# A decoder layer whose five engines get a new order of calls, with scores, norms and one cast written in another form

## The reference

```python
h = layernorm(x)                                   # self-attention: 16 heads of 16, rotary, causal
q, k, v = h @ Wq.T, h @ Wk.T, h @ Wv.T             # 256 x 256 each
x = x + softmax(mask(rope(q) @ rope(k).T / 4)) @ v @ Wo.T
h = layernorm(x)                                   # cross-attention: 16 heads of 64
Q, K, V = h @ W_Q, ctx @ W_K, ctx @ W_V            # 256 -> 1024
s = where(mask, -1e9, Q @ K.T / 8)                 # 256 x 77 for each head
x = x + softmax(s) @ V @ W_O
h = layernorm(x)                                   # FFN, weights rounded to 8 bits by one scale each
h = gelu(h @ q8(W_fc).T + b_fc + 2 * (h @ A_fc.T) @ B_fc.T)          # 256 -> 1024
x = x + h @ q8(W_proj).T + b_proj + 2 * (h @ A_proj.T) @ B_proj.T    # 1024 -> 256
```

## Time and profile before

| what | value |
|---|---|
| three runs | 632.3, 636.84, 644.2 us; median 636.84 |
| profiled execution | 640.39 us, span 638.6 us, mean granted TensorE clock 0.942 |
| TensorE | busy 528.9 us, 83% of the span, 4334 matmuls |
| VectorE, ScalarE, GpSimd | busy 394.3 (62%), 301.3 (47%), 249.0 us (39%) |
| DMA | 62.45 MB; share of 16 engines 34.8% in the SP queue |
| chain that ended last | PE 54%, DVE 23%, ACT 8%, issue 5%, DMA 5%, POOL 3% |

### The profile page before, as it was taken

How to read it: one execution, slowest core, us unless ns; L and a number is a source line. 1 busy time by engine, 2 the same in 40 slices (tenths; PEclk the granted TensorE clock), 3 DMA queues, 4 the chain that set the end, 5 groups by cost and what they waited for, 6 DMA issues and landing times.

```text
span 638.6 us, 11817 instructions
## 1 busy us (share of the span) xinstructions
PE 528.9 (83%) x4334; PEld 449.0 (70%) x4334; DVE 394.3 (62%) x1093; ACT 301.3 (47%) x484; POOL 249.0 (39%) x317
## 2 busy tenths in 40 slices
PE   2488779877987889889988997899899899957955
PEld 2376666665867767878778776878887687846755
DVE  4657622488867963796388548954983683554332
ACT  2323344432362765166535654663556277426323
POOL 5820021455256355155252526272465016522210
PEclk9779986987797999999999999999999999989969
DMA  5598997966040414051315232325140601111000
GB/s 186 167 233 174 193 216 143 225 218 205 26 100 1 150 34 121 1 160 52 88 49 147 61 83 72 89 60 118 37 112 19 157 22 42 37 41 38 1 16 17
DMA packets 63709, 62.45 MB, mean 98 GB/s; under 512 B 6868, under 2 KB 60804, under 8 KB 63652
## 3 DMA queue, kind: packets, MB, share of 16 engines
q1 hardware_dynamic: 62148, 56.74, 34.8%
q0 software_dynamic: 1504, 4.95, 2.2%
HBM read 38.28 MB, written 23.10 MB: 96 GB/s over the span
## 4 chain that ended last, share of the span: by engine, by line
PE 54%; DVE 23%; ACT 8%; issue 5%; DMA 5%; POOL 3%; SPq 1%; DVEq 0%; ACTq 0%; POOLq 0%
PE banks L798 9%; PE banks L799 8%; PE banks L800 8%; PE banks L958 5%; DVE banks L2382 4%; PE banks L1049 4%; PE banks L1060 4%; PE banks L935 4%; PE banks L1122 2%; DMA x_in<-in_x 2%; PE banks L972 2%; ACT probs L1752 2%; DMA fold_raw<-fold_dram 2%; DVE hid_lo L2337 2%; PE banks L832 1%
## 5 line engine op out<-in xcount | busy, mean ns | idle before, releaser
L2382 DVE CUSTOM_DVE_ANT_0 banks<-banks,causal_qk 128x256 f32<-128x256 f32 (+1 forms) x256 | 84.1, 388 | 13.0 <-PE banks L935 11.2
L582 POOL TENSOR_SCALAR_AFFINE_SELECT probs<-probs 128x256 f32<-128x256 f32 x128 | 52.2, 435 | 70.1 <-ACT probs L1752 70.1
L565 POOL TENSOR_TENSOR work<-work,rc 128x616 f32<-128x616 f32 x32 | 40.5, 1266 | 99.7 <-DVE rc L2482 99.7
L1752 ACT ACTIVATE probs<-banks 128x768 f32<-128x768 f32 x64 | 51.7, 808 | 32.5 <-PE banks L958 31.8
L1720 ACT ACTIVATE work<-banks 77x512 f32<-77x512 f32 (+1 forms) x72 | 43.2, 600 | 48.4 <-PE banks L1049 44.0
L572 POOL TENSOR_TENSOR fold_lo<-fold_raw,fold_hi 128x616 fp32r<-128x616 f32 x32 | 48.6, 1523 | 43.4 <-ACT fold_hi L1720 43.4
L2480 DVE TENSOR_REDUCE sm<-work 128x8 f32<-128x616 f32 x32 | 25.4, 793 | 51.0 <-ACT work L1782 50.9
L935 PE MATMUL banks<-k_stack,q_stack 96*128 96x256 f32 (+1 forms) x256 | 42.0, 288 | 13.0 <-DVE mneg L2382 9.7
L958 PE MATMUL banks<-q_stack,k_stack 100*128 100x128 f32 (+1 forms) x256 | 47.1, 309 | 5.7 <-DMA q_stack<-mnegT 2.7
L935 PEld LDWEIGHTS banks<-k_stack,q_stack 96*128 96x128 f32 x256 | 36.2, 197 | 20.2 <-DVE mneg L2382 11.6
L2337 DVE TENSOR_TENSOR late<-banks,late 128x512 fp32r<-128x512 f32 x40 | 27.4, 684 | 35.0 <-ACT late L1720 35.0
(11 more groups left out here) (190 smaller groups left out, 1574.7 us busy)
## 6 DMA issues: line engine op xcount, KB each, us to landing
fold_raw<-fold_dram SPq DMA_DIRECT2D x32, 308.0 KB, 3.1
fold_dram<-work SPq DMA_DIRECT2D x8, 616.0 KB, 8.5
rot_dram<-rot_s_hi SPq DMA_DIRECT2D x16, 256.0 KB, 3.0
rot_dram<-rot_s_lo SPq DMA_DIRECT2D x16, 256.0 KB, 2.8
q_stack<-rot_dram SPq DMA_DIRECT2D x32, 128.0 KB, 2.7
k_stack<-rot_dram SPq DMA_DIRECT2D x32, 128.0 KB, 3.0
fold_dram<-fold_raw SPq DMA_DIRECT2D x4, 616.0 KB, 6.1
fold_dram<-fold_raw_hi SPq DMA_DIRECT2D x4, 616.0 KB, 8.4
```

The lines of the kernel that those rows point to most:

```text
L582: last = pool.affine_select(out=diagonal, in_=diagonal, compare_op=ALU.is_ge, fill=0.0, base=0, pattern=[[0, 2], [1, P]], channel_multipli ...
L1752: act.activation(probs[:, n:n + 2, :], bank[:, 0:2, P:4 * P], ACT.Exp, scale=SCALE).then_inc(p_ok, 1)
L2382: last = dve.tensor_tensor_reduce(out=held[:, at], in0=held[:, at], in1=bias, scale=-1.0, scalar=HUGE, op0=ALU.add, op1=ALU.min, accum_out ...
```

## The change

Four edits.

1. `scores` writes both heads with one matmul for each half of the queries: 512 columns (2 heads x 256 keys) into one bank, 256 columns (2 heads x 128 keys) into the other. `maxima(a, h)` follows: an even h takes the two 256-wide halves, an odd h the two 128-wide ones. The number of its instructions and their widths are the same in sum.
2. `norm` (all three layer norms) is one scalar_tensor_tensor whose second operand is the inverse deviation as a broadcast tensor, in place of a tensor_scalar with two per-partition scalars.
3. The first step of `split_max` is a tensor_tensor (maximum of the tensor with itself), in place of a tensor_copy.
4. The lists of calls of all five engines are in a new order. Line numbers of the new kernel are lower by one from `scores` on, and higher by two or three behind `maxima`.

```diff
@@ -928,12 +928,11 @@
                     pe.wait_ge(stack_ld[1], 16 * STACK_DMAS * (a + 1))
                 if g == 6:
                     pe.wait_ge(mT_ok, 2 * a + 1)
-                banks = (score_bank(2 * g), score_bank(2 * g + 1))
                 for q in (1, 0):
-                    for p in range(2):
-                        keys_q = (q + 1) * P
-                        mm = pe.matmul(halves(banks[p])[:, 1 - q, 0:keys_q], q_stack[0:BOTH, g, q * P:(q + 1) * P],
-                                       k_stack[0:BOTH, g, p, 0:keys_q], start=(q == 1), stop=(q == 0), skip_group_check=True)
+                    keys_q = (q + 1) * P
+                    dst = bank[:, score_bank(2 * g + 1 - q), 0:2 * keys_q].rearrange("p (h n) -> p h n", h=2)
+                    mm = pe.matmul(dst, q_stack[0:BOTH, g, q * P:(q + 1) * P], k_stack[0:BOTH, g, :, 0:keys_q],
...
@@ -2329,8 +2328,9 @@
                 st_ok, mv_ok, rs_ok, xn_ok = sems
                 dve.wait_ge(rs_ok, n + 1)
                 for q in range(QT):
-                    last = dve.tensor_scalar(xn[:, q, :], src[:, q, :], mv[:, q, 0:1], rs[:, q, :],
-                                             ALU.subtract, ALU.mult)
+                    last = dve.scalar_tensor_tensor(out=xn[:, q, :], in0=src[:, q, :], scalar=mv[:, q, 0:1],
+                                                    in1=rs[:, q, :].broadcast_to([P, D]),
+                                                    op0=ALU.subtract, op1=ALU.mult)
                 last.then_inc(xn_ok, 1)
 
             def low(dst, src, hi, done):
...
@@ -2376,12 +2376,14 @@
                     dve.wait_ge(s_ps, HH * a + h // 2 + 1)
                 if h == 0:
                     dve.wait_ge(m_split, 4 * a)
-                held = bank[:, score_bank(h), 0:3 * P]
-                for row, (at, bias) in enumerate(((slice(0, 2 * P), causal_qk[:].rearrange("p a n -> p (a n)")),
-                                                  (slice(2 * P, 3 * P), causal_qk[:, 1]))):
-                    last = dve.tensor_tensor_reduce(out=held[:, at], in0=held[:, at], in1=bias, scale=-1.0, scalar=HUGE,
+                row = h % 2
+                n = (2 - row) * P
+                bias = causal_qk[:, row:].rearrange("p a n -> p (a n)")
+                for p in range(2):
+                    held = bank[:, score_bank(h), p * n:(p + 1) * n]
+                    last = dve.tensor_tensor_reduce(out=held, in0=held, in1=bias, scale=-1.0, scalar=HUGE,
                                                     op0=ALU.add, op1=ALU.min,
-                                                    accum_out=mneg[:, row, h % 2, h // 2:h // 2 + 1])
+                                                    accum_out=mneg[:, row, p, h // 2:h // 2 + 1])
                 last.then_inc(s_max, 1)
 
...
@@ -2390,7 +2392,8 @@
                 dve.wait_ge(s_max, H * a + HH * (half + 1))
                 if a > 0:
                     dve.wait_ge(mT_ps, 2 * a + half - 1)
-                dve.tensor_copy(mneg_s[:, half, :, :, 0, :], mneg[:, :, :, part]).then_inc(m_split, 1)
+                dve.tensor_tensor(mneg_s[:, half, :, :, 0, :], mneg[:, :, :, part], mneg[:, :, :, part],
+                                  ALU.max).then_inc(m_split, 1)
                 dve.wait_ge(m_split, done + 1)
                 low(mneg_s[:, half, :, :, 1, :], mneg[:, :, :, part], mneg_s[:, half, :, :, 0, :], m_split)
```

The new order, by its parts that are spoken of below. SP's list in set-up:

```diff
@@ -380,125 +380,125 @@
 
             first_input()
             weight(QKV_W)
-            trig_tables()
             shift_rows()
             weight(WK_W)
             weight(CTX_W)
+            trig_tables()
             load_x(1)
             weight(WQ_W)
+            weight(WV_W)
             store_rotated(0)
             stacks(0, 0)
             stacks(0, 1)
-            weight(WV_W)
+            load_mask(0)
             residual_input(0)
+            load_x(2)
             weight(WO_W)
-            load_mask(0)
             store_fold(0)
             store_fold(1)
             store_fold(2)
-            load_x(2)
             shifts(0, 0)
             store_fold(3)
             store_fold(4)
             store_fold(5)
             shifts(0, 1)
-            store_rotated(1)
             store_fold(6)
             store_fold(7)
             weight(PJ_W)
+            weight(WO2_W)
+            lora_columns()
             load_fold(0, 0)
             load_fold(0, 1)
-            weight(WO2_W)
+            store_rotated(1)
+            load_mask(1)
             stacks(1, 0)
-            lora_columns()
             stacks(1, 1)
             load_fold(0, 2)
             context_values(0)
```

GpSimd (`split_lo(WO2_W)`), TensorE in set-up, and VectorE at batch 0:

```diff
@@ -612,95 +612,94 @@
...
             store_values(0)
             store_values(1)
             store_values(2)
             store_values(3)
             store_values(4)
+            fold_lo(0, 0)
             inverse_deviation(rs_b, lnb_ve, lnb_rs, 0)
             fold_lo(0, 1)
+            split_lo(WO2_W)
             rotate(2, 0)
             normalise(0, 0)
             rotate(2, 1)
             fold_lo(0, 2)
             fold_lo(0, 3)
             normalise(0, 1)
-            split_lo(WO2_W)
-            normalise(0, 2)
             causal(1, 0)
             causal(1, 1)
...
@@ -1200,32 +1199,32 @@
             fold_keys(6, 1, 0)
-            shifted(0, 3)
             fold_keys(6, 1, 1)
             keys(7, 0)
+            shifted(0, 3)
             weigh(0, 0)
+            keys(7, 1)
+            fold_keys(7, 0, 0)
             shifted(0, 4)
-            keys(7, 1)
-            shifted(0, 5)
-            fold_keys(7, 0, 0)
             fold_keys(7, 0, 1)
             fold_keys(7, 1, 0)
+            fold_keys(7, 1, 1)
+            shifted(0, 5)
             weigh(0, 1)
             shifted(0, 6)
-            fold_keys(7, 1, 1)
             weigh(0, 2)
...
@@ -2575,225 +2578,225 @@
             statistics_b(0)
             xaT_part(2)
             scale(1, PJ_W)
+            quantise(1, PJ_W, 0)
             norm_b(0)
             rotary(2, 0)
             xbT_part(0)
-            quantise(1, PJ_W, 0)
+            quantise(1, PJ_W, 1)
             rotary(2, 1)
             softmax2(0, 0)
             maxima(1, 0)
             sums2(0, 0)
-            quantise(1, PJ_W, 1)
             maxima(1, 1)
             maxima(1, 2)
```

TensorE, from batch 3's projections into batch 2's cross-attention (`scores2(2, g)`, `transpose2(2, g, c)`, `weigh2(2, g)`):

```diff
@@ -1236,428 +1235,428 @@
...
             project_v(3)
+            transpose_f(1)
             project(4, 0)
+            narrow(1)
+            project(4, 1)
+            hidden(1, 0)
             transpose_b(2)
-            transpose_f(1)
-            project(4, 1)
-            scores2(2, 0)
             scores(3, 0, 5)
-            narrow(1)
             scores(3, 1, 5)
-            hidden(1, 0)
             hidden(1, 1)
             scores(3, 2, 5)
-            scores2(2, 1)
+            hidden(1, 2)
             scores(3, 3, 5)
-            hidden(1, 2)
             scores(3, 4, 5)
+            scores2(2, 0)
             hidden(1, 3)
             transpose_max(3, 0)
             scores(3, 5, 5)
+            scores(3, 6, 5)
             project_down(1, 0)
-            scores(3, 6, 5)
-            transpose2(2, 0, 0)
-            transpose2(2, 0, 1)
             scores(3, 7, 5)
             project_down(1, 1)
-            weigh2(2, 0)
-            scores2(2, 2)
-            transpose2(2, 1, 0)
+            scores2(2, 1)
             transpose_max(3, 1)
             shifted(3, 0)
+            shifted(3, 1)
+            transpose2(2, 0, 0)
+            shifted(3, 2)
+            transpose2(2, 0, 1)
+            shifted(3, 3)
+            weigh(3, 0)
+            weigh2(2, 0)
+            shifted(3, 4)
+            scores2(2, 2)
```

1128 lines of the change are left out of this document (562 added, 566 removed).

## The result

The changed kernel takes 655.87 us, the median of 4 runs (655.5 to 658.02), against 637.07 before (4 runs, 632.3 to 644.2). The ratio is 1.032, 95% interval 1.0275 to 1.0364: 3.2% slower. The profiled execution is 655.56 us, its span 653.7, the mean granted clock 0.920 (0.942 before).

A forecast was written before the change was run, and what follows sets the result against it. TensorE was taken as the bound, busy 528.9 us and idle 109.7. The terms summed to -14 us, from 640.4 to 626.4 us for the profiled execution, 623 us on the median; range 606 to 642.

The forecast's parts named there:

- T4: First `shifted` at 90 us: more work ahead of a 2.68 us wait and less half clock behind it, -4 us.
- T6: TensorE's 2.79 us wait at 196 us, at `transpose_f(0)`: more work ahead of it, half clock behind it partly saved, -4 us.
- T7: Steady state, 206 to 564 us: some of 35.5 us of idle goes, -3 us, bounds -9 and +6.
- T9: A new stall where a long GpSimd instruction meets a short VectorE one: +2 us for one chance in three.
- T1: Scores: a group takes 0.35 us instead of 0.41, partly offset by longer waits for maxima; sum -2 us.
- T2: Norms and cast with two tensor operands: no escape from GpSimd's lock, 0 us, bounds -16 to +2.
- T3: Start: the split of the context comes earlier, the rotary tables later; +1 us, between -3 and +4.
- T5: Split of WO2_W moved: 3.14 us wait and half clock behind it go, -7 us; collision ahead of `rotate(2, 0)`, +4.
- A: Rival: stalls move, the DMA-bound stretch takes back the gain at 90 us, WO2_W's split costs more; 632 us, chance 0.27.
- B: Rival: batch 2's cross-attention is squeezed, TensorE waits 5 us four times and the clock falls; 647 us, chance 0.11.
- C: Rival: two-operand norms and cast on VectorE escape GpSimd's lock; 608 us, chance 0.10.
- D: Rival: a group of wide scores still takes 0.41 us and waits 0.11 us more for its bank; 632 us, chance 0.05.

The follow-up runs named there:

- hyb_middle: Kernel before with the new order of calls only from 253 to 390 us, old forms of scores, norms and cast: 642.35 us, ratio 1.0137.
- b_scores_1: Kernel before with only the wide scores and their maxima, in the old order: 636.65 us, ratio 0.9975.
- b_operands_1: Kernel before with only the two-operand norms and cast, in the old order: 641.4 us, ratio 1.005.
- b_fill: Kernel before with unread matmuls in three TensorE waits, ahead of transpose_f(0), transpose_b(7) and transpose_f(7): 637.18 us, ratio 1.0015.
- b_scores_wo2: Kernel before with wide scores and GpSimd's split of WO2_W moved between fold_lo(0, 2) and fold_lo(0, 3): 637.08 us, ratio 0.9973.
- hyb_late: Kernel before with the new order of calls only from 390 us on, old forms of scores, norms and cast: 643.35 us, ratio 1.012.
- a_wo2: Changed kernel with the split of WO2_W and the quantisation back in their old places: 657.17 us, ratio 1.0309 to the kernel before.
- a_fill: Changed kernel with unread matmuls in four places where TensorE waits for a norm: 653.17 us, ratio 1.025 to the kernel before.
- order_spread: Kernel before with the new order alone, scores2(2, 1) moved behind shifted(3, 1) on TensorE: 650.21 us, ratio 1.0219.
- order_alone_1: Changed kernel with the three other edits undone, so the new order of calls alone: 651.33 us, ratio 1.011 to the kernel before.

## Why the prediction was wrong

The forecast was 623 us in a range of 606 to 642, and faster by 2.2%; it is slower by 3.2%. Two steps failed: T4 to T6 priced waits, and half clock behind them, that the order could not turn into time, and T7 and T9 left new falls of the clock in the steady part out of the sum. The second is the larger in size. By its own terms:

- **T1 fits.** A group of scores takes 0.35 us, in the changed kernel's timeline of TensorE the distance of two starts:

```profile
420.26 0.51 PE L934 MATMUL banks<-k_stack,q_stack 96*128 96x512 f32 x2
420.61 0.65 PE L1048 MATMUL banks<-ident,work 128*77 128x128 f32 x4
```

and the waits for maxima rose from 9.7 us to 13.7, in the old order to 11.6, a rise of 1.9 where 1.7 was forecast.

```profile
PE banks L934 <- DVE mneg L2384: 13.7, 17, 1.6
```

-2 us forecast, ratio 0.9975 (-1.6 us, interval -3.4 to +0.3) measured in the old order. In the new order the wide scores came with more lost clock (above).

- **T2 was mis-sized.** The mechanism held (no escape from GpSimd), but the bound of +2 us was too low. It took the price of a two-tensor instruction from the maxima, which read PSUM. In the changed kernel the norms are (min/median/max ns)

```profile
L2331 DVE SCALAR_TENSOR_TENSOR xn_a<-x_in,mv_a,rs_a x16: 445/572/4643, 9.5 to 433.1; 128x256 f32<-128x256 f32 x16
L2331 DVE SCALAR_TENSOR_TENSOR work<-x,mv_b,rs_b x16: 472/481/1637, 132.9 to 581.8; 128x256 f32<-128x256 f32 x16
```

481 ns undisturbed: 72 ns x 48 = 3.5 us, and the measured cost is 3.2 us (1.005) in the old order and 5 us in the new, where the median of the first group is 572 ns. The prediction put 0 in its sum.

The Trainium skill, "VectorE: DVE Perf Modes", section "The perf-mode tier table", has a float32 tensor_scalar in SBUF about twice as fast as a tensor_tensor at 2048 elements. That 409 ns becomes 481 with the scalar_tensor_tensor of this case has its sign; the factor at 256 elements is 1.18.

- **T3 to T6, the early part, -10 us forecast, +2.7 measured (1.0042, interval -0.5 to +5.9).** The new places were read rightly. T3's wait for the split of the context grew from 6.5 to 8.1 us. T5's collision came as foreseen:

```profile
127.38 4.52 POOL L542 TENSOR_TENSOR wo_lo<-wo_raw,wo_hi 128x2048 fp32r<-128x2048 f32 x1
127.63 5.36 DVE L2275 TENSOR_SCALAR wpj_raw<-wpj_raw,winv 128x2048 f32<-128x2048 f32 x1
...
132.91 0.87 DVE L2331 SCALAR_TENSOR_TENSOR work<-x,mv_b,rs_b 128x256 f32<-128x256 f32 x2
...
133.84 0.90 PE L1013 MATMUL banks<-ident,work 128*128 128x128 f32 x3 [5.06 <-DVE work L2331]
```

The quantisation takes 5.36 us instead of 1.79 beside GpSimd's 4.52, and `transpose_b(0)` waits 5.06 us behind it. What failed is the price of the gains. T4 took -4 us from a wait of 2.68 us and the 17.1 us at half clock, but the long half clock and most of the wait belonged to this execution and not to the kernel. In hyb_middle, which has the same old order there, the wait is 0.4 us and the same stretch is at 0.90:

```profile
90.00:107.00 17.00, 14.93 (x115) 10.87 (x115) 4.28 (x4) 8.92 (x14) 4.10 (x8) 0.90 0.99 205
```

In five more kernels with the old order there (b_scores_1, b_operands_1, b_fill, b_scores_wo2, hyb_late) 84 to 107 us is at 0.85 to 1.00 and the wait between nothing and 2.0 us, and the changed kernel's 0.85 is no better.

T5 took -7 us and T6 -4 for waits that end and the clock behind them. b_scores_wo2 ends exactly T5's wait and gains 1.6 us at the place and nothing that can be measured in the time; b_fill takes away the half clock behind T6's wait and gains nothing. **This is the step that failed first: "such a wait costs itself and as much again behind it".** In its place the runs showed that the waits next on the chain take half of it back, and that the clock falls nearby whether or not this wait stands there. T6's own wait, at `transpose_f(0)`, is 0.91 us in the changed kernel instead of 2.79, and half clock is there all the same, behind the wait of the next point.

- **A place that the prediction did not see.** In the changed kernel `scores(2, 0)` stands right behind `project(3, 1)`, and it waits until the rotary has read those banks (its `wait_ge` on `trig`), and the rotary comes behind GpSimd's `rotate`, which must have read `probs` first:

```profile
192.77 0.69 DVE L2369 TENSOR_TENSOR probs<-banks,cos_t 128x512 f32<-128x512 f32 x1
...
194.14 0.72 POOL L550 TENSOR_TENSOR rot<-probs 128x256 f32<-128x256 f32 x1 [0.53 <-DVE probs L2369]
194.82 0.72 POOL L551 TENSOR_TENSOR rot<-probs 128x256 f32<-128x256 f32 x1
...
195.65 0.69 DVE L2369 TENSOR_TENSOR probs<-banks,cos_t 128x512 f32<-128x512 f32 x1
196.25 0.68 DVE L2369 TENSOR_TENSOR probs<-banks,sin_t 128x512 f32<-128x512 f32 x1
...
197.04 0.70 PE L934 MATMUL banks<-k_stack,q_stack 96*128 96x512 f32 x2 [3.00 <-issue]
```

The row puts the 3.00 us down to "issue", since no event in the trace names the releaser; the `wait_ge` and the times do: the second rotary ends at 196.93 (196.25 + 0.68). Half clock follows from 197 to 205 us. Before, `hidden(0, 0)` and `transpose_b(1)` stood between. A wait for a bank to be handed back does not show in the list of instructions, only in the `wait_ge` of the call.

- **T7 and T9 failed in sign and size.** The steady state was given -3 us (at most +6) and new stalls +2 us, because 35.5 us of idle time seemed to be what an order can change. Measured: +8.7 us in the middle (1.0137) and +7.6 us in the late part with the tail (1.012), which has T8 too; by mean spans 6.6 and 5.5. What the prediction left out of this stretch is the clock. The one execution shown was at 1.00 from 206 to 564 us, so T7 was counted in idle time alone; no term allowed for more half clock than one new stall would bring. Full clock all through was luck of that execution (0.97 or 0.98 in five other kernels with the old order). The lost clock of the changed kernel is 16.8 us more in the mean, that of hyb_middle 10.5. For the late part the clock is not what failed: against the kernel before beside it hyb_late has 0.5 us less lost clock and 6.0 us more of the rest, where T7 had the idle time shrink.

- **The rivals.** A gave 632 us. B gave 647 with a reach of 640 to 660, and the result lies in it, but not by B's mechanism: B has TensorE wait 5 us four times in batch 2's cross-attention, and the longest wait at L1048 for a normalised group is 0.9 us. B had the place (falls at 282 and 293 us), and "a clock that falls at several new places" stood among the prediction's own signs of being wrong. C fell in both orders. D fell with b_scores_1.

**Open.** Where the new order's middle loses clock is shown (282 to 310 and 330 to 352 us), why it falls there is not, and why its late part loses time otherwise is not settled either. What each fall costs was measured for none of them alone. Three single repairs (a_wo2, a_fill, order_spread) each changed the place that they aimed at and left the mean span within 3 us. No version was faster than the kernel before beyond its interval.

## What to carry to other kernels

Before pricing the removal of a wait, look what the next wait on its chain is: here the end of a wait of 3.2 us brought 1.6 us at the place and nothing measurable in the whole. Do not sum against one execution where the clock falls at different places in different runs. Compare span and mean clock of all of them, and the same stretch in traces of near relatives of the kernel: the 17 us of half clock at 90 us stood in one trace only, those at about 150 us in the trace of every kernel with the old order there. A reordering that leaves all work in place can still lose by 3%, spread over the program, with waits of 2 us at most in the steady part: give such a change a range that reaches as far to the slower side as to the faster one.

## What the runs showed of the hardware

- The same program (order_alone_1) differs by 15.6 us of span between two of its ten runs with an equal rest (604.3 and 604.0 us): between these two the granted clock alone makes the difference. Over the 74 runs of the kernel before, span rises by 0.50 us for each us of lost clock (correlation 0.86), in the ten of order_alone_1 by 0.85. A reading of this, not tested: the part that does not show in the span falls into waits that would have been there anyway.
- Unread matmuls in a wait (a_fill) kept the clock at 1.00 for the 11 us from 128 to 139 us, and then it was at 0.53 for 18 us, longer than without them.
- The maxima, which read PSUM and one tensor in SBUF, take 0.42 us beside a GpSimd subtraction of 4.57 us (b_scores_wo2), as without it (443 ns); the cast and the two-tensor maximum, which read only SBUF, wait for its end (4.19 and 3.82 us).
- A norm with its second operand as a broadcast tensor in SBUF takes 480 ns for 256 elements, 409 with a per-partition scalar; both wait until a long GpSimd instruction ends (4245 and 4129 ns at the longest, beside one of 4.51 us).
